# Attention stage: a chunk's four exponentials ahead of the q copies on ScalarE, and the row places behind the statistics and first input on VectorE

## What is computed

```python
ln1 = _layer_norm(hidden_states, ln1_weight, ln1_bias)
qkv = jnp.einsum('sbh,oh->sbo', ln1, qkv_weight)
...
scores = jnp.where(causal, scores, jnp.finfo(scores.dtype).min)
attn = jax.nn.softmax(scores, axis=-1)
ao = jnp.einsum('bgqst,bgtd->bgqsd', attn, vb)
...
h1 = hidden_states + proj
ln2 = _layer_norm(h1, ln2_weight, ln2_bias)
logits = x @ router_weight
top_p, top_i = jax.lax.top_k(probs, K)
...
padded_tokens = jnp.zeros((T, H), x.dtype).at[dst].set(x[order // K], mode='drop')
```

## Time and profile before

| | us |
|---|---|
| median of 3 runs | 4695.05 (4687.83 to 4703.43) |
| the profiled execution, its own time | 4694.2 |
| its span, first to last instruction | 4692.6 |
| attention, slots 2 to 31 | 1017 of the span |
| TensorE busy in the span | 4084.0 (87%) |
| VectorE busy in the span | 3868.6 (82%) |
| ScalarE busy in the span | 2676.8 (57%) |
| GpSimd busy in the span | 2214.4 (47%) |

### The profile page before, as it was taken

The page is one execution under the profiler, slowest core; times in us unless marked ns, Lnnn a source line. Parts: engine busy times, 40 slices in busy tenths (PEclk is TensorE's granted clock), DMA queues, the critical chain, the costliest instruction groups (busy, mean ns, idle before and its releaser), DMA issues. The chain is left out here.

```text
span 4692.6 us, 75960 instructions
## 1 busy us (share of the span) xinstructions
PE 4084.0 (87%) x20868; PEld 3138.8 (67%) x20869; DVE 3868.6 (82%) x7673; ACT 2676.8 (57%) x4136; POOL 2214.4 (47%) x1865
## 2 busy tenths in 40 slices
PE   5989998999999999999997888888888189888988
PEld 3666666666666666666665676767666189888988
DVE  6999999999999999999997666666667277777777
ACT  4666676666666667666765555555555043434343
POOL 2444444434343434343435355555555445555555
PEclk7888888888888888888888888887888599999999
DMA  2111010111010101111111122222222345445554
GB/s 59 30 27 35 26 35 26 35 26 38 24 37 24 38 28 32 30 30 30 30 30 38 62 74 83 77 78 76 84 84 76 105 76 92 82 89 87 85 87 75
DMA packets 181894, 255.69 MB, mean 54 GB/s; under 512 B 22881, under 2 KB 126690, under 8 KB 181858
## 3 DMA queue, kind: packets, MB, share of 16 engines
q1 hardware_dynamic: 120930, 157.20, 11.7%
q0 software_dynamic: 60928, 98.09, 10.9%
HBM read 138.63 MB, written 116.59 MB: 54 GB/s over the span
## 5 line engine op out<-in xcount | busy, mean ns | idle before, releaser
L539 PE MATMUL pj<-xt,win 128*128 128x512 f32 x3144 | 982.5, 469 | 51.6 <-DVE xt L708 37.2
L539 PEld LDWEIGHTS pj<-xt,win 128*128 128x128 f32 x3144 | 685.0, 221 | 281.1 <-issue 85.3
L294 POOL TENSOR_TENSOR wk<-v,uc 128x512 f32<-128x512 f32 x260 | 334.3, 1286 | 694.1 <-DVE v L770 693.6
L1942 POOL DMA_INDIRECT out<-e_y,e_to x272 | 445.4, 1637 | 426.4 <-DVE e_y L2089 355.2
L587 PE MATMUL po<-yz,wout 128*128 128x512 f32 x1024 | 484.5, 629 | 72.2 <-DVE h1o L857 44.8
L721 DVE SCALAR_TENSOR_TENSOR uc<-pj,convw,uc 128x511 f32<-128x511 f32 (+2 forms) x780 | 518.4, 730 | 13.5 <-ACT uc L360 13.5
L1992 PE MATMUL e_p<-e_w,e_a 128*128 128x256 f32 x3264 | 421.5, 287 | 43.1 <-DVE e_a L2082 43.1
L1980 PE MATMUL e_p<-e_xt,e_w 128*128 128x256 f32 x3264 | 411.5, 283 | 39.0 <-DVE e_xt L2070 38.0
L1992 PEld LDWEIGHTS e_p<-e_w,e_a 128*128 128x128 f32 x3264 | 401.9, 195 | 44.7 <-DVE e_a L2082 44.7
L1980 PEld LDWEIGHTS e_p<-e_xt,e_w 128*128 128x128 f32 x3264 | 392.0, 189 | 48.0 <-issue 47.3
L587 PEld LDWEIGHTS po<-yz,wout 128*128 128x128 f32 x1024 | 199.2, 200 | 310.0 <-issue 309.1
(11 more groups left out here) (247 smaller groups left out, 9292.0 us busy)
## 6 DMA issues: line engine op xcount, KB each, us to landing
e_x<-expert_in SPq DMA_DIRECT2D x137, 260.0 KB
bb<-bc SPq DMA_DIRECT2D x65, 512.0 KB, 4.8
a_h<-h_rows SPq DMA_DIRECT2D x136, 128.0 KB
h_rows<-h1o SPq DMA_DIRECT2D x32, 512.0 KB, 5.5
a_hb<-h_rows SPq DMA_DIRECT2D x128, 128.0 KB
out<-a_bs SPq DMA_DIRECT2D x128, 128.0 KB
bc<-xd SPq DMA_DIRECT2D x65, 128.0 KB, 2.2
e_w1s<-in_moe_w POOLq DMA_DIRECT2D x10, 512.0 KB
```

The source lines that it names most:

```text
L294: pool.tensor_tensor(wk[:, m, :], v[:, m, :], uc[d][:, m, :], ALU.mult).then_inc(S["dtu_ok"], 1)
L539: i = mm(pj[m][:], win[d][wp][:, k, c:c + P], xt[xp][:, k, :], start=(k == 0 and n == 0), stop=(k == KD - 1 and n == 2))
L1942: pool.indirect_dma_start(out=out, out_offset=bass.IndirectOffsetOnAxis(ap=to[n][:, j:j + 1].bitcast(U32), axis=0), in_=y[n][:, j, :], in_ ...
```

## The change

It reorders calls in two of the `slot` functions of `attention_stage`, and nothing else. On ScalarE exponentials 2 and 3 stand ahead of the four q copies instead of behind them. On VectorE `stats1(c+2)` and `first_input(c)` stand ahead of `keep_logits`, `next_rows` and `place` instead of behind them. `pick_experts` and `normalise` stay last.

```diff
@@ attention_stage, act: slot(c)
                 exp(c, 1)
                 if not (isinstance(c, int) and c < 2):
                     second_odds(c - 2)
+                exp(c, 2)
+                exp(c, 3)
                 for q in range(NQ):
                     q_copy(c + 1, q)
-                exp(c, 2)
-                exp(c, 3)
@@ attention_stage, vector: slot(c, p)
                 sums(c)
+                stats1(c + 2)
+                first_input(c)
                 if not first:
                     keep_logits(c - 1)
                     if not (isinstance(c, int) and c < 2):
                         next_rows(c - 2)
                         place(c - 2, p)
-                stats1(c + 2)
-                first_input(c)
-                if not first:
                     pick_experts(c - 1)
                 normalise(c + 2)
```

## The result

The changed kernel takes 4828.14 us (median of 4 runs, 4820.83 to 4845.12), the kernel before 4699.24 us in the same comparison (4 runs, 4687.83 to 4707.65). The ratio is 1.028, 95% interval 1.0248 to 1.0312. That is 68 us above the forecast and 3 us above the range. The sign was right, the size was half of what came. The changed kernel was timed in one of the two, and there the change costs nothing (ratio 1.0005).

The account below looks back on a forecast made before the run. Attention slots were taken as bound by a loop through the burst's held TensorE signals: legs 17.75 + 17.6 = 35.35 us, taken as 34.9 against 32.66. Thirty slots add 66 us to 4694.2, giving 4760, range 4670 to 4825.

Parts of the forecast that it names:

- the hold: TensorE's semaphores rise late behind GpSimd's burst of eight scattering transfers, until 11.8 us behind the burst's start.
- The loop of scores, burst and held signals: Attention slot: delivered scores to next burst, then burst to next delivered scores; 19.32 and 11.8 us before the change.
- ScalarE's half, 2.2 us later: Attention slot: q copies behind exponential 3 start `x2t` 2.2 us later, moving the router and TensorE's work behind it.
- The router's duration: Term between `x2t` copies and GpSimd's copy and places: 2.4 us, between 1.95 and 2.75.
- The burst's start: GpSimd: copy and places remain behind the router, 1.86 us, so the burst starts 4.56 us earlier against TensorE's work.
- Leg A: From delivered scores to the next burst: 17.75 us forecast against 19.3 before.
- The extrapolated series: Banks of `products` behind the burst's start: first free, second let through at 3.6, third 7.8, fourth 11.8 us.
- Leg B: From the burst's start to the next delivered scores: 17.6 us forecast against 11.8 before.
- low clock all along: Rival: TensorE stays at 1.2 GHz from router and `turn_p` on, 4827 us; chance 0.08.
- VectorE's half: Statistics and first input, 3.35 us, cover the wait before the logits' copy; alone worth 0, but the burst moves earlier.
- The hold passes the products: Rival: products and projection finish within the burst, a slot takes 31.8 us, 4669 in all; chance 0.25.
- The parts cancel: Rival: no change, leg B 14.9 and leg A 17.75, third bank passing near 7.8, fourth near 10.5; chance 0.14.

Follow-up runs that it names:

- one of the two: Two of five later comparisons, where TensorE's signals weren't held; kernel before 4596.38 and 4600.46 us; the changed kernel ran in the latter, 4599.38 us.
- the first comparison: Changed kernel, both halves, against the kernel before: 4828.14 against 4699.24 us, ratio 1.028.
- the five later ones: Follow-up comparisons of the halves, added waits, moved loads and left-out or split scatters with the kernel before, which took 4596.38 to 4708.01 us.
- The version that gained 1% here: Kernel before plus VectorE's half, with GpSimd waiting for the second bank of products ahead of its scatters: ratio 0.9898, then 0.9945 and 1.0029.
- Two groups of four transfers: Changed kernel, with GpSimd waiting for the chunk's fourth bank of products between two groups of four scatters: 4595.21 us, 0.9979 of the kernel before.
- the last comparison with the hold: Kernel before 4704.74 us, changed kernel 4829.75 us, ratio 1.0284; VectorE's half with GpSimd's wait for the second bank 4673.49 us.

## Why the prediction was right in its sign and wrong in its size

The kernel took 4828 us where 4760 was forecast, with a range of 4670 to 4825. Two steps failed. The third bank of products was to pass the hold at 7.8 us, and passed at 11.7 with the fourth. And the router was to take 2.4 us, and took 3.58.

**What bounds the kernel: right, with a condition unknown to it.** The loop of scores, burst and held signals describes both traces of the first comparison. That the signals are late doesn't follow from the program alone. With the same instructions the hold was there in the first comparison and in three of the five later ones, and absent in two. The prediction set a page beside it: by the Trainium skill (TensorE: Matmul & The Clock Gate, The cost: per-tile semaphore tail) increments cost about 26 ns each, so nothing would be held. The two comparisons without the hold don't contradict the page: no wait is marked remote, and eight `ao` copies run in one row. The rows are too coarse to show 26 ns. The other four comparisons show delays of several us.

**ScalarE's half, 2.2 us later: right.** From the end of the last subtraction to the first `x2t` copy it is 3117.12 - 3114.09 = 3.0 us, where it was 0.8. TensorE waits 2.74 us for `x2t` where it waited 0.89, and without scatters the two kernels differ by 2.3 us a slot.

**The router's duration: mis-sized.** I took 2.4 us from between 1.95 and 2.75. It takes 3.58 here and in about two thirds of the slots. The granted clock was 1.00 from 3108.0 to 3115.6, ahead of the 2.74 us of idle time, and 0.50 over the router, from 3118.6 to 3122.2, which is the lower level of 1.2 GHz. The idle time alone doesn't settle it: six routers behind the same 2.74 us took 1.95. The low clock was said to be a rival with a chance of 0.08.

**The burst's start: mis-sized by 0.7.** It was to be 0.15 us behind the last place. The places end at 3123.91, the burst starts at 3124.70. Leg A from row to row is 3124.70 - 3105.81 = 18.9 us against 17.75 forecast. The router adds 1.2, the start 0.7, and the subtractions take off 0.8, since they end 8.3 us in and not 9.1.

**The extrapolated series: right in kind, wrong in its second and third member.** The second bank was to pass at 3.6. "The third at 7.8, the fourth at the end, 11.8." Measured, the second comes at 5.8, the third and fourth together at 11.7. So not a quarter but half of the projection stands behind the hold, and at a low clock (0.62 from 3137.2 to 3143.0): 3.78 us against 0.9 to 1.9. Leg B is 3143.46 - 3124.70 = 18.8 us against 17.6. This step and the router's clock are what failed: 37.6 us in this slot where 34.9 was forecast for the mean, which came out as 36.5 since some slots are shorter. The rival "low clock all along" gave 4827, 1 us from the result, and part of that is luck: it had the low clock, but a router of 2.75 us and only a quarter of the projection behind the hold.

**VectorE's half: what it does through the burst was seen, what it does for VectorE was missed.** Under the hold this half costs 0.5% by the burst's place. Without the hold it takes away VectorE's wait for the tile that the scatters read, which the prediction didn't look at. What that is worth alone wasn't measured.

**The rivals.** "The hold passes the products" fell in the first trace, by 33 waits of the `ao` copies. "The parts cancel" is the outcome of the comparison without the hold, but not for the reason given there, which was a bank that passes the hold earlier.

## What to carry to other kernels

Edits that cost half a per cent each can cost three together when they decide what lies in a stall of fixed length. Look at what each engine waits for in that window, not at instruction counts. Where a delay shows up as a late signal and not as late work, time the same pair of kernels again, at another time and on another chip, before building on it. The version that gained 1% here gained 0.5% in a second comparison and lost 0.3% where the stall was absent. Two groups of four transfers gave 0.998, but were never timed with the stall present. A series guessed from one spacing deserves both its ends in the range.

## What the hardware showed unexpectedly

Behind GpSimd's eight indirect transfers TensorE's semaphore rises were held until 11.7 us behind the start of the first, behind four until 5.8 us. Its matmuls went on: the four banks of `products` were read in by 5.7 us. No wait for another engine's signal is marked remote. The loads of `h1` aren't needed for the hold. With the same program it was present in four comparisons (before at 4699 to 4708 us) and absent in two (4596 and 4600 us), and always the same within a comparison. What sets it is open. The record gives the number 5 for the chip of the last comparison with the hold and of the last one without it, timed 13 minutes apart. If that number names one and the same chip, the chip alone doesn't set it, and the core's place or its neighbours are left; no run tells. Whether splitting the burst helps where the hold is present wasn't measured, since that comparison had no hold.
